# Early gathers by halves of groups, and other orders in the message stage

## What is computed

```
for l in 3: h = h @ Ws_self[l] + mean over edges(h[src] by dst) @ Ws_neigh[l] + b   (relu between)
x = layernorm(x + h)
hs, hv = x[:, :128] @ w_s, x[:, 128:] @ w_v           # 4 x 32 numbers per node: "message table"
W = (softplus(f @ W1 + b1) - log 2) @ W2 + b2, times rcut          # filters, per edge
edge = products of (hs, hv)[dst of the edge], its direction and W
agg = segment_sum(edge, src of the edge)
x = layernorm(x + second_layer(softplus(agg @ wf1)...))
```

## Time and profile before

| | us |
|---|---|
| median of 3 runs (lowest, highest) | 2094.54 (2092.11, 2095.12) |
| the profiled execution, its own time | 2094.46 |
| its span in the trace | 2092.6 |
| PE, DVE, ACT, POOL busy | 1906.2, 1289.1, 594.7, 1079.9 |
| mean granted clock of PE | 0.956 |

### The profile page before, as it was taken

How to read it: one execution, slowest core, us unless ns; L and a number is a source line. 1 busy time by engine, 2 the same in 40 slices (tenths; PEclk the granted TensorE clock), 3 DMA queues, 4 the chain that set the end, 5 groups by cost and what they waited for, 6 DMA issues and landing times. The chain is left out here.

```text
span 2092.6 us, 23699 instructions
## 1 busy us (share of the span) xinstructions
PE 1906.2 (91%) x8445; PEld 1216.9 (58%) x8445; DVE 1289.1 (62%) x1985; ACT 594.7 (28%) x1380; POOL 1079.9 (52%) x1054
## 2 busy tenths in 40 slices
PE   7799999999999999999999999999837778888886
PEld 3344455555555555555555566666635567676775
DVE  6899989677763343333333355555325688878785
ACT  1355532100000000000000001111225566676773
POOL 4000000000047888788887874288777777666660
PEclk9899999999999999999999999999869899999997
DMA  4255444322223333333322247356423333232330
GB/s 141 65 176 187 172 153 167 117 87 88 88 85 95 99 111 101 106 94 95 95 94 80 74 158 243 116 187 208 141 91 99 114 88 109 82 98 81 98 91 20
DMA packets 111705, 240.15 MB, mean 115 GB/s; under 512 B 28358, under 2 KB 51811, under 8 KB 111584
## 3 DMA queue, kind: packets, MB, share of 16 engines
q1 hardware_dynamic: 77008, 179.10, 26.2%
q0 software_dynamic: 34576, 59.48, 10.2%
HBM read 163.76 MB, written 74.72 MB: 114 GB/s over the span
## 5 line engine op out<-in xcount | busy, mean ns | idle before, releaser
L1057 PE MATMUL low<-table,abuf 125*125 125x512 f16 x3750 | 844.0, 380 | 4.8 <-DVE abuf L1497 4.8
L1057 PEld LDWEIGHTS low<-table,abuf 125*125 125x125 bf16 x3750 | 505.3, 137 | 300.4 <-issue 28.0
L901 PE MATMUL mid<-wbuf,h_t 128*125 128x512 f32 x1200 | 560.0, 603 | 5.4 <-DVE st_out L1539 3.8
L789 POOL DMA_INDIRECT by_src<-scat_row,sort x416 | 490.0, 1178 | 126.1 <-issue 118.8
L794 POOL DMA_INDIRECT table<-msg_table,wbuf x300 | 317.8, 1059 | 137.3 <-issue 82.5
L1091 PE MATMUL low<-table,wbuf 128*125 128x256 f32 x900 | 255.5, 443 | 121.8 <-DVE table L1785 121.8
L901 PEld LDWEIGHTS mid<-wbuf,h_t 128*125 128x125 f32 x1200 | 215.1, 190 | 210.5 <-issue 200.4
L781 POOL TENSOR_TENSOR scat_row<-scat_row 128x64 f32<-128x64 f32 x26 | 16.0, 617 | 558.1 <-DVE sort L1659 557.5
L1091 PEld LDWEIGHTS low<-table,wbuf 128*125 128x125 f32 x900 | 196.1, 221 | 171.1 <-DVE table L1785 132.3
L1497 DVE TENSOR_TENSOR abuf<-abuf,row_scale 125x3125 bf16<-125x3125 bf16 (+3 forms) x84 | 256.5, 3059 | 3.4 <-DMA abuf<-adj 3.4
L1546 DVE SCALAR_TENSOR_TENSOR y<-low,inv_deg,st_in 125x512 f32<-125x512 f32 x75 | 56.3, 750 | 328.1 <-PE low L1057 210.9
(11 more groups left out here) (210 smaller groups left out, 1717.3 us busy)
## 6 DMA issues: line engine op xcount, KB each, us to landing
abuf<-adj SPq DMA_DIRECT2D x75, 781.2 KB, 4.7
adj<-table SPq DMA_DIRECT2D x25, 781.2 KB, 4.6
states<-st_out SPq DMA_DIRECT2D x75, 256.0 KB, 2.0
st_in<-states SPq DMA_DIRECT2D x75, 256.0 KB, 4.7
early_rows<-sort POOLq DMA_DIRECT2D x25, 384.0 KB, 3.0
table<-early_rows SPq DMA_DIRECT2D x25, 384.0 KB, 6.0
by_src<-scat_row,sort POOLq DMA_INDIRECT x416, 2.2
by_src<-blank SPq DMA_DIRECT2D x25, 252.0 KB, 4.4
```

Source lines behind the costliest of these rows:

```text
L789: pool.indirect_dma_start(out=by_src, out_offset=bass.IndirectOffsetOnAxis(ap=place_i[:, k * PIECE + j:k * PIECE + j + 1], axis=0), in_=sc ...
L901: last = pe.matmul(to[0:TN, :], h_t[i % 2][:, k, :], weights[l % 2][:, a, k, :], start=k == 0, stop=k == KC - 1)
L1057: last = pe.matmul(p_agg[k % 2][0:TN, :], a_tile[k % 3][:, a, :], table[ps % 2][0:TN, a, h, :], start=a == 0 and h == 0, stop=a == TILES - ...
```

## The change

The early gathers are split in halves of a group: first slots 0 to 2 of all 25 tiles, two tiles per store (13 steps), then slots 3 to 5 of the first 20 tiles (10 steps), then group 1 of tile 0 into a tensor of its own. Each of the three has its own needed number of table tiles and its own wait. The three pairs of tiles left get their second halves in tiles 4, 8 and 12 of the message stage. Index loads read only the slots used. `early_max` moves from iteration 60 to 57, the transpose from 61 to 58, `early_need` from 62 to 58. `filt_h` gets a second buffer. In the message stage PE does `output_1(t-1)` before `sums(t, 2)`; ACT does `output_1(t-1)` last in the tile and `root(t-1)` before `scaled(t, 2)`. A path for inputs with edges out of range of the fast form (`general_planes`) stores whole tiles; its lines have no instruction in the trace.

```diff
-            def load_early(t):  (POOL)
+                slots = slice(0, GS if t else 2 * GS)
+                pool.dma_start(win_p[t % 3][:, slots, :],
+                               by_src[t * WIN:(t + 1) * WIN, :].rearrange("(p j) k -> p j k", j=SLOTS)[:, slots, :])
...
+            def gather_early(p, half):
+                s = early_step(p, half)
+                if s >= 3:
+                    pool.wait_ge(s_est[s % 3], loads_of(s - 3, 3))
+                for t in early_tiles(p):
+                    for j in range(HALF):
+                        gather_slot(s, t % 2 * HALF + j, e_idx[:, t, half * HALF + j:half * HALF + j + 1])
+            def store_early(p, half):
+                pool.wait_ge(s_eg[s % 3], early_gathered(s))
+                pool.dma_start(early_rows[2 * p * P:(2 * p + n) * P, half * HALF * G:(half + 1) * HALF * G]...)
...
-            need = pool.value_load(e_need[0:1, 0:1], min_val=1, max_val=TILES)
-            wait_alone(pool, s_rows, need)
-            for t in range(EARLY):
-                gather_early(t)
-                if t:
-                    store_early(t - 1)
-            store_early(EARLY - 1)
+            needs = [pool.value_load(e_need[0:1, n:n + 1], min_val=1, max_val=TILES) for n in range(3)]
+            wait_alone(pool, s_rows, needs[0])
+            for p in range(PAIRS):
+                gather_early(p, 0)
+                if p:
+                    store_early(p - 1, 0)
+            wait_alone(pool, s_rows, needs[1])
+            for p in range(PROMPT):
+                gather_early(p, 1)
+                store_early(p - 1, 1) if p else store_early(PAIRS - 1, 0)
+            wait_alone(pool, s_rows, needs[2])
+            gather_second()
+            store_early(PROMPT - 1, 1)
+            store_second()
...
 SP, ahead of the message stage's loop:
             load_early(0)
+            sp.wait_ge(s_est[SECOND % 3], loads_of(SECOND, 3))
+            sp.dma_start(msg_slots[0][:, GS:2 * GS, :], second_rows.rearrange("p (j k) -> p j k", j=GS)).then_inc(s_second, 16)
...
 PE:
+                if t >= 1:
+                    output_1(t - 1)
                 sums(t, 2)
-                if t >= 1:
-                    output_1(t - 1)
...
 ACT:
                 scaled(t, 0)
-                if t >= 2:
-                    output_1(t - 2)
...
+                if t >= 2:
+                    root(t - 1, s_ovar, s_orstd)
                 scaled(t, 2)
                 if t + 2 < TILES:
                     features(t + 2)
-                if t >= 2:
-                    root(t - 1, s_ovar, s_orstd)
-            output_1(TILES - 2)
+                if t >= 1:
+                    output_1(t - 1)
...
 DVE:
             def hidden(t):
                 dve.wait_ge(s_mact, 3 * t + 3)
-                if t:
-                    dve.wait_ge(s_w2, NG * t)
-                dve.scalar_tensor_tensor(out=filt_h[0:BLK * F, :, :], ...
+                if t >= 2:
+                    dve.wait_ge(s_w2, NG * (t - 1))
+                dve.scalar_tensor_tensor(out=filt_h[t % 2][0:BLK * F, :, :], ...
...
-                if k == 60:
+                if k == 57:
                     early_max()
-                if k == 62:
+                if k == 58:
                     early_need()
```

More of the change, by code:

```diff
@@ L21 @@
 GS = 6
+HALF = GS // 2
 NG = SLOTS // GS
@@ L154, in gnn_kernel @@
     e_idx = early.take(P, [TILES, GS], I32)
[L155 to L159, removed]
+    e_second = early.take(P, [GS], I32)
+    e_f = early.take(P, [2, TILES, HALF])
+    e_fs = early.take(P, [GS])
+    e_max = early.take(P, [3])
+    e_most = early.take(1, [3])
+    e_below = early.take(1, [3, TILES])
+    e_need = early.take(1, [3], I32)
     tot = sb("tot", [P, BINS])
@@ L251, in gnn_kernel @@
     m_exp = wreg.take(P, [NBLK, P])
-    filt_h = wreg.take(P, [NBLK, P])
+    filt_h = [wreg.take(P, [NBLK, P]) for _ in range(2)]
     feat_t = wreg.take(P, [NBLK, P])
@@ L435, in loads_of, with early_tiles, early_step, early_gathered @@
         return 16 * (i // bufs + 1)
+    def early_tiles(p):
+        return range(2 * p, min(2 * p + 2, TILES))
+    def early_step(p, half):
+        return p if half == 0 else PAIRS + p + (p >= PROMPT)
+    early_count = {SECOND: GS}
+    early_count.update({early_step(p, half): HALF * len(early_tiles(p)) for p in range(PAIRS) for half in range(2)})
+    def early_gathered(s):
+        return 16 * sum(early_count[n] for n in range(s % 3, s + 1, 3))
+    def slots_gathered(t, g):
+        if g == 0:
+            return 16 * (t // 2 + 1)
+        return 16 * GS * (t // 2 + (0 if g == 1 and t % 2 == 0 else 1))
     def node_rows(t):
@@ L845, in _ @@
                 pool.wait_ge(s_win[t % 3], loads_of(t, 3))
[L846 to L850, removed]
+                late = [p for p in PAIRS_AT if PAIRS_AT[p] == t]
+                for p in late:
+                    gather_early(p, 1)
+                for g in range(1 if t else 2, NG):
+                    if g == 2:
+                        for p in late:
+                            store_early(p, 1)
                     if t >= 2:
@@ L1042, in _ @@
                         bin_sums()
-                    if k == 61 and a == 4:
+                    if k == 58 and a == 4:
                         pe.wait_ge(s_emax, 1)
-                        pe.transpose(p_b[0][0:1, 0:P], e_max[:, :], ident[:, :]).then_inc(s_emt, 1)
+                        for n in range(3):
+                            top = pe.transpose(p_b[0][0:1, n * P:(n + 1) * P], e_max[:, n:n + 1], ident[:, :])
+                        top.then_inc(s_emt, 1)
                     if k == AGGS - 3 and a == 8:
@@ L1079, in filters @@
                     pe.wait_ge(s_w_free, n - 1)
-                filter_products(p_w[n % 2], [filt_h[0:BLK * F + 1, GS // BLK * g + b, :] for b in range(GS // BLK)], CUTS).then_inc(s_w2, 1)
+                filter_products(p_w[n % 2], [filt_h[t % 2][0:BLK * F + 1, GS // BLK * g + b, :] for b in range(GS // BLK)], CUTS).then_inc(s_w2, 1)
             def sums(t, g):
@@ L1743, in _ @@
                     dve.wait_ge(s_ps, AGGS)
-                    dve.memset(filt_h[BLK * F:BLK * F + 1, :, :], 1.0)
+                    for b in range(2):
+                        dve.memset(filt_h[b][BLK * F:BLK * F + 1, :, :], 1.0)
                 if k == AGGS - 1:
```

69 lines of the change are left out of this document (46 added, 23 removed).

## The result

| | before | after |
|---|---|---|
| median, us (lowest to highest, runs) | 2094.74 (2092.11 to 2095.12, 4) | 1992.41 (1991.83 to 1993.22, 4) |
| the profiled execution, its span | 2094.46, 2092.6 | 1993.22, 1991.4 |
| mean granted clock of PE | 0.956 | 0.978 |

The ratio is 0.9514, with a 95% interval of 0.9498 to 0.9531: 102 us less, at 1992.4 against a forecast of 1992. A median that close is partly luck.

What follows compares the result with a forecast made beforehand. POOL's gathers were taken as the bound: loop's first gather at 1533.5, 430 us of gathers to 1963.5, last group near 1965, tail 25, span 1990, plus 1.86 beside the span: 1992 us (48%), range 1968 to 2035.

Steps and rivals of the forecast that it cites:

- The bound: Message stage after the change: POOL's 309 gathers at 1.385 us and 3 stores, 430 us, set the end.
- The start: Third pass: need known in iteration 58, first early gather at 1300.5, 47 us earlier, with no PE stall taken.
- The stores: POOL before the loop: 24 stores instead of 20, half-length pieces taken to add 0, bounds 0 and 14 us.
- The loop: PE and DVE in the message stage: period falls from 20.36 to 16.70 us a tile.
- All three terms: Message loop, per tile: `output_1` off the path 0.88, second `filt_h` 1.10, last sums at the upper clock 1.68 us.
- The tail: From DVE's start on the last group to the span's end: 25 us instead of 28.4, bounds 23 and 28.4.
- DVE and PE bound throughout: Message stage: gathers stay at 1.35 or less, so DVE and PE, not POOL, set the end: 1975 us; 13%.
- Another wait at 20 us a tile: Message loop: another wait takes the old loop's place, only the start gains: 2062 us; 6%.
- a first gather that stays late: Third pass: first gather not early though the need is known, from register loads or late table tiles: +20, 2012 us; 3%.
- The lower clock stays: Last sums of each tile in the message loop: lower clock remains, period 18.4, 2015 us; 12%.
- The copies no earlier: Third pass: POOL's index copies end no earlier, PE stalls 10 to 12 us in iteration 58: 2003 us; 15%.
- The slower case: Message loop: PE waits for ACT's `output_t` before the last sums; at a period of 22 the time is 2102 us; 3%.

Runs made afterwards that it cites:

- five kernels: Changed kernel (1992.41 us); it with the need in iteration 62 (2031.09), all stores on SP (1978.35), second group gathered directly (1991.03); earlier kernel with new loop orders (2025.02).
- gap filled: The kernel before the change plus four matmuls with zeros in PE's idle slot before the last sums of each tile: 2066.90 us.
- `output_1` behind: The changed kernel with `output_1` behind the last sums on PE and behind the first scaling on ACT, as before: 2016.48 us.
- old hidden wait: The changed kernel, but the hidden layer's step on DVE waits for all filters of the tile before, as with one buffer: 2014.33 us.
- gathers only: The changed kernel with PE's and ACT's orders and the hidden layer's wait of before: 2053.20 us.

## Why the prediction was right, step by step

**The bound.** Right up to tile 15, and beyond it not shown. DVE waits for gathers up to 1803.67, and extra gathers in the early tiles cost their full time. POOL's sum also comes out: the forecast's 456.5 us from the first gather of the loop to the end of the span is 454.9 in the trace. The chain of gathers is full from 1536.49 to 1962.69, 426.2 us (forecast 430) for 309 gathers and 3 stores. A gather costs 1.073 plus 0.30, where I had taken 1.385 at a full DVE. In the last ten tiles DVE runs without a wait, and the last group starts 3 us after its rows can be there, at 1968.39 (forecast 1965). There 12 gathers of 1.373 are 16.5 and the period is 16.58, so the two bounds coincide, and it is partly luck that pricing the end by POOL alone came so close.

**The start.** Forecast 1300.5, measured 1302.62. The third pass was 2.4 late in iteration 58 (1292.32 against 1289.93 in the earlier trace rows), and had been since its first tile (1219.92 against 1217.49), where nothing of the change acts yet. The way from the need to the first gather took 2.75 (taken 3.5). The copies ended at 1289.31, 0.8 late, and the largest index left DVE in time for PE: no stall. DVE waited 2.84 for it, in a slot where it idles anyway.

**The stores.** The one term mis-sized by its nearest row. I had put "bounds 0 and 24 x 0.59 = 14 us more, nearest row the store itself, so 0". A pair's store takes 0.75 to 0.78 against 0.59, 3.8 us over the 22 such stores ahead of the loop. The odd tile's store, with half as many pieces, took 0.58. The chain from the first early gather to the last store's end took 232.2 against 231: stores 3.8 more, and 2.6 less in the rest, most of it in the lengthened gathers (37 instead of 39.3). The loop's first gather came at 1536.5, not 1533.5, most of it from the late start.

**The loop.** Forecast 16.70, measured 16.58. All three terms came as priced, and each was measured alone. But the condition given for the clock, a gap of 2.37 us that did no harm, was too simple: after gaps of 1.9 the lower clock came in about every second tile. Had the gap closed to 1.9 only, the forecast would have missed by 0.8 us in each tile and I would have called it safe.

**The tail.** 23.0 us; taken 25, bound 23. The last sums ran at the upper clock. The last `output_2` did not: it took 2.04 at 1981.74 where the one before took 1.04.

**The late pairs.** The forecast held them as part of POOL's sum. They show as three long tiles, 22.8 us in all, close to 15 gathers of 1.373 and three stores.

**The rivals.** DVE and PE bound throughout: refuted, since DVE waits for gathers until tile 15 and the tiles with late pairs take 22 to 25 us; in the last ten tiles it holds as well as POOL's sum. Another wait at 20 us a tile, and a first gather that stays late: refuted, by 16.58 and 1302.62. The lower clock stays: refuted in the changed kernel, real at gaps of 1.9. The copies no earlier: refuted, 33.3 against 43.3 us. The slower case, PE waiting for ACT before the last sums: PE waits there for DVE alone, 0.68 to 1.61 us from tile 1 on where no gathers are late.

## What to carry to other kernels

When one engine's queue is full from one point to the end, price every edit in that engine's microseconds, before the loop as well as in it. Here five kernels whose loops started up to 50 us apart agreed in the time behind that start within 5 us. When two bounds lie close, edits to both add up, and each alone shows which bound it leaves. Before an engine's long instruction is called free because it idles afterwards, look at whose instruction it holds up: cutting one of 3.4 us into four returned 20 us of another engine's chain, though no run here could show these 20 us in the time.

## What the runs showed of the hardware

The twelve matmuls of the last sums, by the idle time of PE before them, in every tile in which it lay in the range given:

| idle before, us | kernel | at 4.1 to 4.5 us (lower level) |
|---|---|---|
| 0.7 to 1.4 | changed | 0 of 18 |
| 1.05 to 1.4 | gap filled | 0 of 20 |
| 1.56 to 1.59 | `output_1` behind | 1 of 18 |
| 1.89 to 1.97 | old hidden wait | 10 of 19 |
| 2.78 to 2.85 | gathers only | 18 of 20 |
| 2.78 to 2.83 | before | 15 of 16 |

The share rises with the idle time, and in between the tiles mostly alternate, one at the lower level and one at the upper. Single tiles go against it: with the old hidden wait 1.61 us came before the lower level, and 2.22 and 2.58 before the upper one. The Trainium skill, TensorE: Matmul & The Clock Gate, HAM oscillation, ties the fall to longer gaps than any of these; the rows disagree. Its section "A second HAM failure mode: psum-queue depth-cycling" tells of frequent short idles that do the same, and the alternation agrees with that one. To run 1.89 us of products with zeros in the idle time returned 1.66 us in each tile.

A store issued by POOL cost 0.58 with 128 pieces and 0.75 to 0.78 with 256 of the same size.

A gather that meets one bf16 instruction of DVE of 3.41 us takes 2.3 to 4.1 us (15 of them in the changed kernel, most 3.4 to 3.6); those that meet quarters of it take 1.1 to 1.8.
